# First attention of a two-layer kernel: VectorE's maxima over two banks at a time, a new order of the engines, and a re-ordered preparation

## Chip, core and metric

The kernel runs on one core of one Trainium2 chip. The metric is the device time of one execution in microseconds, the median of several runs. One further execution was recorded by the hardware profiler.

## What is computed

The reference is two transformer layers with cross-attention and feed-forward parts over x of 8 x 256 x 256 and a context of 8 x 1601 x 64. The change touches the first cross-attention alone:

```python
q_big  = rope(einsum('bshk,hkq->bshq', (x @ Wq.T).reshape(B, S, H, K), w_kc_q))   # H=16, K=128, q: 192
kv_r   = rope(kv_c)                                                               # 8 x 1601 x 64
q_r    = einsum('bshq,hqr->bhsr', q_big, W_qr)
k_r    = einsum('bld,hdr->bhlr', kv_r, W_kr)
scores = einsum('bhsr,bhlr->bhsl', q_r, k_r)
attn   = softmax(scores)
ctx_c  = einsum('bhsl,bld->bhsd', attn, kv_r)
out    = einsum('bhsd,hkd->bhsk', ctx_c, w_kc_kv) ... @ Wo.T
```

There are 8 batches x 16 heads = 128 heads, each with 256 query rows against 1601 keys. The kernel folds W_qr and W_kr into one matrix M per head, and w_kc_kv and Wo into one matrix per head (wvo).

## The kernel before

**Preparation** (`phase_prepare`). SP loads weights, x and the context. TensorE makes Wq x w_kc_q per head, transposes x, folds M and wvo. ScalarE copies results out of PSUM, takes the norms (lines 351 to 356) and splits weights into a high and a low float16 part. VectorE takes the largest absolute value of each batch of context (`top_of`, line 421), normalises x (lines 452 to 463), makes the low parts (`split_rest`, line 434) and applies the rotation to batches 5, 6 and 7 of the context (`turn_context`, lines 439 to 442); GpSimd rotates batches 0 to 4. VectorE's order at the end is: `split_rest` of 16 heads, the copy of the norms (line 482), `turn_context(5)`, the bounds and the scaling of M (line 494), the scale of the keys (lines 500 to 505), `turn_context(6)` and `(7)`. ScalarE takes the square root that normalises x after head 7 (line 356). SP stores M to DRAM in six pieces (lines 222 to 226), then wvo, 1 MB, to a DRAM scratch (line 231), and waits for that store (line 234) before the stage may end; all engines meet at the end of a stage.

**First attention** (`phase_attention0`). The order of every engine is written out by hand, in a loop over four heads, which is software-pipelined: while head n has its values summed, head n+1 has its scores made and head n+2 its maxima taken. Per head:

- TensorE, `maxima` (line 767): q (float16, 128 queries as weights) times all keys, in 4 chunks of 400 or 401 keys x 2 halves of the queries, 8 products, each into one of the two banks of `psM`, by turns. VectorE, `reduce_max` (line 1053), takes the maximum of each product: 8 reductions of 128x400. A product waits for the reduction two before it (`mx_done`), so one bank is filled while the other is read.
- VectorE, `join` (lines 1062 to 1070), joins the maxima into a column `mcol`; TensorE, `shift` (line 771), turns it by one 64-column transpose; ScalarE, `shift_copy` (line 935), puts it into rows of q2, so that the score products subtract it.
- TensorE, `scores` (line 783): 26 products of 256 columns in groups of 4, 4, 4 and 1 key tiles, into `psS[0]` and `psS[1]` by turns; the last group's tile has 65 keys, so its weights have 65 columns. ScalarE, `exp` (line 947), takes the exponential of a group. GpSimd (line 1152) makes the low part.
- TensorE, `values` (lines 801 and 804): 26 pairs of products of 129 and 65 columns, accumulated into `psV`; ScalarE copies it to `acc` (line 1002), SP stores it (line 684).
- Every two heads TensorE makes a new pair of queries: `q_first` (12 products, line 729), `q_second` (6), `q_lat` (float32, line 754), with the rotation by VectorE between them (lines 1012 to 1037), and the copies `q_high`, `q_other` (ScalarE, 923 and 930) and `q_low` (VectorE, 1044).

The transposed column and the joined maxima stand in the spare columns of `psM`'s second bank. Before the loop, the keys are transposed by TensorE (`turn_keys`, line 817) and copied by ScalarE (line 958), VectorE makes the values' low parts (`v_rest`, line 1076), and SP fills the buffers: `refill_maxima` is one DMA for each chunk (line 593). The rule that paces the maxima is this one:

```python
                if not (isinstance(n, int) and n == 0 and k < ST):
                    pe.wait_ge(mx_done, PASSES * n + k - 1)      # PASSES = 8, k = 0..7
```

## Time and profile before

| | us |
|---|---|
| three runs | 1766.52 to 1771.66, median 1769.66 |
| the profiled execution, its own time | 1781.06 |
| its span, first to last instruction | 1779.2 |
| first attention's loop, first to last copy of a head's result | 121.0 to 1193.3 |

| engine | busy us (share) |
|---|---|
| TensorE (PE) | 1653.8 (93%) |
| VectorE (DVE) | 1328.9 (75%) |
| ScalarE (ACT) | 1015.1 (57%) |
| GpSimd (POOL) | 925.9 (52%) |

PE is a matmul's record, PEld the load of its weights, SPq the SP engine's queue as it issues DMAs. A matmul's record runs from its start to the arrival of its last column, so records overlap: the pace of TensorE is read from start to start. A timeline row with "x6" merges six instructions, from the start of the first to the end of the last.

### The profile page before, as it was taken

The numbers are of one execution on the slowest core, as the hardware profiler recorded it, in microseconds if no ns is written. First come the engines' busy times: TensorE is split into PE (matmuls) and PEld (weight loads), VectorE is DVE, ScalarE is ACT, GpSimd is POOL, SyncE is SP. The second block draws the span as 40 slices with busy tenths as digits, with TensorE's granted clock in tenths as the row PEclk, the third lists the DMA queues.
The fourth block names the chain that finished last, engine by engine and source line by source line (L and its number), as shares of the span: only waits on it lengthen the run. The fifth ranks groups of instructions, "written<-read, shape, count | busy, mean of one in ns | idle before, by whom it ended". The sixth has DMA issues, their size and how long they took to land. (4 is left out here: it accounts for less than half of the span.)

```text
span 1779.2 us, 48732 instructions
## 1 busy us (share of the span) xinstructions
PE 1653.8 (93%) x16216; PEld 1326.5 (75%) x16216; DVE 1328.9 (75%) x2910; ACT 1015.1 (57%) x2028; POOL 925.9 (52%) x623
## 2 busy tenths in 40 slices
PE   5789999999999999999999999989777799987898
PEld 4568888888888888888888888868655455557776
DVE  5788888888888888888888888886564378874223
ACT  5676666666666666666666666652122266662111
POOL 5337777777777777777777777760002122111321
PEclk8699999999999999999999999999988899997999
DMA  9621121221221121121121142139300000004244
GB/s 261 232 80 51 58 85 50 58 81 50 61 77 53 57 83 52 58 83 52 55 83 53 52 128 79 56 98 315 92 11 23 21 13 12 12 7 172 93 140 146
DMA packets 150154, 144.14 MB, mean 81 GB/s; under 512 B 41306, under 2 KB 137224, under 8 KB 149600
## 3 DMA queue, kind: packets, MB, share of 16 engines
q1 hardware_dynamic: 148432, 139.56, 25.9%
q0 software_dynamic: 1536, 3.99, 0.6%
q8 instruction: 23, 0.38, 0.1%
q14 instruction: 19, 0.16, 0.0%
q10 hardware_dynamic: 144, 0.07, 0.0%
HBM read 91.61 MB, written 33.98 MB: 71 GB/s over the span
## 5 line engine op out<-in xcount | busy, mean ns | idle before, releaser
L1152 POOL TENSOR_TENSOR c_rest<-c_prob 128x1024 f16<-128x1024 f32 (+1 forms) x513 | 796.4, 1573 | 310.9 <-ACT c_prob L947 297.0
L947 ACT ACTIVATE c_prob<-c_psS,ln,c_exp_scale 128x1024 f32<-128x1024 f32 (+1 forms) x514 | 538.1, 1047 | 239.8 <-PE c_psS L783 234.7
L1053 DVE TENSOR_REDUCE c_mxp<-c_psM 128x1 f32<-128x400 f32 (+1 forms) x1040 | 589.4, 573 | 111.2 <-PE c_psM L767 97.0
L783 PE MATMUL c_psS<-c_q,c_kk 128*128 128x256 f16 (+1 forms) x3350 | 512.7, 273 | 0.2 <-issue 0.2
L801 PE MATMUL c_psV<-c_vb,c_prob 128*128 128x129 f16 (+1 forms) x3328 | 396.3, 222 | 0.0
L783 PEld LDWEIGHTS c_psS<-c_q,c_kk 128*128 128x128 f16 (+1 forms) x3350 | 321.9, 99 | 85.7 <-issue 0.4
L804 PE MATMUL c_psV<-c_vb,c_rest 128*128 128x65 f16 (+1 forms) x3328 | 374.1, 193 | 0.0
L767 PE MATMUL c_psM<-c_kkm,c_q 128*128 128x400 f16 (+1 forms) x1040 | 346.1, 333 | 4.8 <-DVE c_mxp L1053 3.0
L804 PEld LDWEIGHTS c_psV<-c_vb,c_rest 128*128 128x128 f16 (+1 forms) x3328 | 301.2, 99 | 22.1
L801 PEld LDWEIGHTS c_psV<-c_vb,c_prob 128*128 128x128 bf16 (+1 forms) x3328 | 305.2, 97 | 14.0
L729 PE MATMUL c_psQ<-c_xb,c_w2s 128*128 128x256 f16 x1188 | 164.1, 275 | 11.6 <-PEq L162 9.9
L1973 ACT ACTIVATE g_prob<-g_psS,g_bias 128x128 f32<-128x128 f32 (+1 forms) x264 | 107.0, 426 | 56.7 <-DVE g_bias L2014 56.7
L729 PEld LDWEIGHTS c_psQ<-c_xb,c_w2s 128*128 128x128 f16 x1188 | 102.9, 98 | 28.5 <-issue 12.7
L1835 POOL TENSOR_TENSOR g_km<-kT,g_hmask 128x1024 f32<-128x1024 f32 x18 | 34.0, 1912 | 157.8 <-PE g_psS L1874 120.1
L767 PEld LDWEIGHTS c_psM<-c_kkm,c_q 128*128 128x128 f16 x1040 | 101.7, 98 | 14.1 <-DVE c_mxp L1053 3.7
L754 PE MATMUL c_psQ<-c_roped,c_ms 128*128 128x256 f32 x396 | 101.5, 392 | 0.6 <-DVE c_roped L1037 0.6
L935 ACT ACTIVATE c_q<-c_psM 32x128 f16<-32x128 f16 x258 | 69.2, 268 | 48.9 <-PE c_psM L771 47.4
L2330 ACT ACTIVATE m_s<-m_psH 128x256 f32<-128x256 f32 (+1 forms) x48 | 18.4, 384 | 113.3 <-PE m_psH L2248 106.1
L923 ACT ACTIVATE c_q<-c_psQ 64x256 f16<-64x256 f32 x132 | 50.0, 379 | 49.9 <-PE c_psQ L754 48.3
L754 PEld LDWEIGHTS c_psQ<-c_roped,c_ms 128*128 128x128 f32 x396 | 70.0, 190 | 7.6 <-DVE c_roped L1037 0.8
L2366 DVE TENSOR_TENSOR m_g<-m_s,m_psH 128x256 f32<-128x256 f32 (+1 forms) x48 | 20.2, 420 | 72.8 <-ACT m_s L2330 68.0
L2014 DVE TENSOR_REDUCE g_bias<-g_psS 128x4 f32<-128x1024 f32 (+1 forms) x49 | 59.9, 1223 | 16.6 <-PE g_psS L1874 13.9
(298 smaller groups left out, 2153.6 us busy)
## 6 DMA issues: line engine op xcount, KB each, us to landing
c_w2s<-w_scr SPq DMA_DIRECT2D x66, 256.0 KB, 2.6
acc_scr<-c_acc SPq DMA_DIRECT2D x128, 129.0 KB, 2.2
c_ms<-m_scr SPq DMA_DIRECT2D x67, 192.0 KB, 2.3
c_w2s<-w_scr SPq DMA_DIRECT2D x66, 128.0 KB, 2.1
kv<-acc_scr SPq DMA_DIRECT2D x4, 2064.0 KB, 9.8
d_acc<-acc_scr SPq DMA_DIRECT2D x4, 2064.0 KB, 8.6
m_w<-in_L_ffn_W SPq DMA_DIRECT2D x16, 352.0 KB, 4.2
c_vb<-V SPq DMA_DIRECT2D x27, 129.0 KB, 2.0
```

Source lines behind the costliest of these rows:

```text
L729: mm = pe.matmul(out, weights[:, w, c], xb[:, x, c, :], start=(c == 0 and i == 0), stop=(c == DK - 1 and i == 2))
L754: mm = pe.matmul(psQ[:, S:2 * S], ms[:, e, :], roped[:, e, :], start=(e == 0), stop=(e == 2))
L767: pe.matmul(psM[:, st, 0:w], q1[slot][:, st * P:(st + 1) * P], kkm[:, c0:c0 + w], start=True, stop=True).then_inc(mx_full, 1)
L783: mm = pe.matmul(psS[g % 2][0:r, i * S:(i + 1) * S], src[:, (lo + i) * P:(lo + i) * P + r], mov[slot][:, :], start=(one == 0 and i % 2 == ...
L801: pe.matmul(psV[:, st * W:(st + 1) * W], high[0:r, c0:c0 + P], vb[0:r, i, :], start=(i == 0 and st == 0), stop=False, skip_group_check=True)
L804: mm = pe.matmul(psV[:, st * W + DC:(st + 1) * W], rest[g][0:r, c0:c0 + P], vb[0:r, i, DC:W], start=False, stop=(i == LT - 1), skip_group_ ...
L935: last = nc.scalar.activation(q2[slot][0:2 * SHIFT_ROWS, st * P:(st + 1) * P], shiftT[st * 2 * SHIFT_ROWS:(st + 1) * 2 * SHIFT_ROWS, :], A ...
L947: nc.scalar.activation(prob[g][0:r, 0:w], psS[g % 2][0:r, 0:w], ACT.Exp, bias=keep["ln1024"][0:r, :], scale=exp_scale[slot][0:r, :]).then_ ...
L1053: nc.vector.tensor_reduce(mxp[:, st, c:c + 1], psM[:, st, 0:CHUNKS[c][1]], AX.X, ALU.max).then_inc(mx_done, 1)
L1152: nc.gpsimd.tensor_tensor(rest[g][0:r, 0:w], prob[g][0:r, 0:w], high[0:r, 0:w], ALU.subtract).then_inc(rest_done, 1)
L1973: ins = nc.scalar.activation(prob[k % 2][:, i * w:(i + 1) * w], psS[k % 2][:, i * w:(i + 1) * w], ACT.Exp, bias=bias[k % 2][:, i:i + 1], a ...
L2014: nc.vector.tensor_reduce(bias[k % 2][:, 0:nh], psS[k % 2][:].rearrange("p (h k) -> p h k", h=nh), AX.X, ALU.max, negate=True).then_inc(bi ...
```

## The change

In the first attention a chunk of maxima is now two products, one into each bank of `psM`, and one reduction over both banks (4 for each head, of 128x2x400). A chunk's products wait for the reduction of the chunk before, so `psM` has no second buffer any more. The column and the joined maxima move to the second bank of `psS[1]`; `join` so waits for an exponential, and the first scores of a head wait for `shift_copy` themselves. The order of all engines in the loop is new. A refill of a chunk of keys is two DMAs of 64 partitions. In the preparation the wvo result stays in SBUF (no DRAM scratch), the square root follows head 3, `turn_context(5)` and the keys' scale come earlier, and the table load for the exponential moves to the end of the preparation.

```diff
@@ phase_prepare
-    wvo = sb("a_wvo", [P, H0 // 2, D])
+    wvo = keep["wvo_made"]
...
             sp.dma_start(keep["ms"][:], ...).then_inc(keep["in_m"], 16)
-            sp.wait_ge(vo_done, N_VO)
-            sp.dma_start(t["wvo_scr"], wvo[:]).then_inc(stored, 16)
...
-            sp.wait_ge(stored, 16 * 2)
+            sp.wait_ge(stored, 16)
...
-                if h == H0 // 2 - 1:
+                if h == 3:
                     act.wait_ge(var_ready, 1)
                     nc.scalar.activation(root[:], agg[:, :, 1], ACT.Sqrt, ...)
...
+            nc.scalar.activation(warm[:], eps[:], ACT.Exp)
...
             for h in range(H0):
                 split_rest(h)
+            turn_context(POOL_TURNS)
             n = D_NM
...
             dve.sem_inc(b2_ready, 1)
-            turn_context(POOL_TURNS)
+            dve.wait_ge(aall_ready, 1)
+            kscale = keep["kscale"]
+            link(nc.vector.tensor_reduce(ktop[:], aall[:], AX.X, ALU.max))
+            link(nc.vector.tensor_scalar(ktop[:], ktop[:], 1e-30, TURN_GROWTH / QK_TOP, ALU.add, ALU.mult))
+            link(nc.vector.reciprocal(kscale[:], ktop[:]))
+            link(nc.vector.tensor_copy(keep["k_unscale"][:], ktop[:]))
             dve.wait_ge(bound_ready, 1)
@@ phase_attention0
-    PASSES = 2 * len(CHUNKS)
+    PASSES = len(CHUNKS)
...
-    shiftT = psM[0:ST * 2 * SHIFT_ROWS, 1, SPARE:SPARE + P // 2].bitcast(F16)
-    mx = psM[:, 1, SPARE + P // 2:SPARE + P // 2 + ST]
+    shiftT = psS[1][0:ST * 2 * SHIFT_ROWS, 512:512 + P // 2].bitcast(F16)
+    mx = psS[1][:, 512 + P // 2:512 + P // 2 + ST]
...
-        queue.dma_start(kkm[:, c0:c0 + w], KK1[:, bass.ds(b * L + c0, w)]).then_inc(in_kkm[c], 16)
+        for half in range(2):
+            rows = slice(half * DC, (half + 1) * DC)
+            queue.dma_start(kkm[rows, c0:c0 + w], KK1[rows, bass.ds(b * L + c0, w)]).then_inc(in_kkm[c], 16)
...
-            def maxima(n, p, k, slot):
+            def maxima(n, p, c, slot):
...
-                    pe.wait_ge(mx_done, PASSES * n + k - 1)
+                    pe.wait_ge(mx_done, PASSES * n + c)
                 c0, w = CHUNKS[c]
-                pe.matmul(psM[:, st, 0:w], q1[slot][:, st * P:(st + 1) * P], kkm[:, c0:c0 + w], ...
+                for st in range(ST):
+                    mm = pe.matmul(psM[:, st, 0:w], q1[slot][:, st * P:(st + 1) * P], kkm[:, c0:c0 + w], ...)
+                mm.then_inc(mx_full, 1)
...
 def scores(n, g, slot, part=None):
+                    if g == 0:
+                        pe.wait_ge(shift_done, n + 1)
...
@@ TensorE's loop, the new order
+                    if u % 2 == 0:
+                        maxima(n + 1, p1, 3, s1)
+                        q_first(p, 0)
+                        scores(n, 2, u, (4, 8))
+                        values(n, 0, (0, 1))
+                        scores(n, 3, u)
+                        maxima(n + 2, p2, 0, s2)
+                        values(n, 0, (1, 2))
+                        values(n, 0, (2, 3), shift_of=n + 1)
+                        shift(n + 1)
+                        q_first(p, 1)
+                        values(n, 0, (3, 4))
+                        values(n, 1, (0, 1))
+                        maxima(n + 2, p2, 1, s2)
+                        values(n, 1, (1, 3))
+                        scores(n + 1, 0, s1)
+                        scores(n + 1, 1, s1, (0, 6))
+                        maxima(n + 2, p2, 2, s2)
+                        values(n, 1, (3, 4))
+                        scores(n + 1, 1, s1, (6, 8))
+                        values(n, 2, (0, 2))
+                        scores(n + 1, 2, s1)
+                        maxima(n + 2, p2, 3, s2)
+                        values(n, 2, (2, 4))
+                        values(n, 3)
+                    else:
+                        q_second(p)
+                        maxima(n + 2, p2, 0, s2)
+                        values(n, 0, (0, 2))
+                        scores(n, 3, u)
+                        values(n, 0, (2, 3), shift_of=n + 1)
+                        shift(n + 1)
+                        values(n, 0, (3, 4))
+                        values(n, 1, (0, 3))
+                        maxima(n + 2, p2, 1, s2)
+                        values(n, 1, (3, 4))
+                        scores(n + 1, 0, s1)
+                        values(n, 2, (0, 1))
+                        q_lat(p)
+                        maxima(n + 2, p2, 2, s2)
+                        scores(n + 1, 1, s1, (0, 2))
+                        values(n, 2, (1, 2))
+                        scores(n + 1, 1, s1, (2, 8))
...
+                        values(n, 3)
@@ ScalarE's loop
+                    exp(n, 2, u)
                     if u % 2 == 0:
-                        q_other((AHEAD // 2) * j + (u + 2) // 2, (u + 2) % AHEAD)
-                    exp(n, 2, u)
-                    shift_copy(n + 1, (u + 1) % AHEAD)
-                    exp(n, 3, u)
-                    exp(n + 1, 0, (u + 1) % AHEAD)
-                    if u % 2 == 1:
+                        shift_copy(n + 1, (u + 1) % AHEAD)
+                        exp(n, 3, u)
+                        exp(n + 1, 0, (u + 1) % AHEAD)
+                    else:
+                        exp(n, 3, u)
+                        shift_copy(n + 1, (u + 1) % AHEAD)
+                        exp(n + 1, 0, (u + 1) % AHEAD)
                         q_high((AHEAD // 2) * j + (AHEAD + u) // 2, u - 1)
...
+                    if u % 2 == 1:
+                        q_other((AHEAD // 2) * j + (AHEAD + u) // 2, u - 1)
@@ VectorE
-                nc.vector.tensor_reduce(mxp[:, st, c:c + 1], psM[:, st, 0:CHUNKS[c][1]], AX.X, ...
+                nc.vector.tensor_reduce(mxp[:, :, c], psM[:, :, 0:CHUNKS[c][1]], AX.X, ALU.max).then_inc(mx_done, 1)
...
+                    if u % 2 == 0:
+                        reduce_max(n + 1, 3)
                     join(n + 1)
+                    scale_of(n + 2, (u + 2) % AHEAD)
                     reduce_max(n + 2, 0)
...
@@ build
+        keep["wvo_made"] = sb(layer0, "wvo_made", [P, H0 // 2, D])
```

In the stage's start, the `v_rest(7)` of VectorE moves behind `join(0)`, the maxima of head 1 end with chunk 2, and `scores(0, 2)` stops after four products instead of six.

## Rows read from the trace of the kernel before

**Rows 1.** The page, part 1: busy time, share of the span, instructions.

```profile
PE 1653.8 (93%) x16216; PEld 1326.5 (75%) x16216; DVE 1328.9 (75%) x2910; ACT 1015.1 (57%) x2028; POOL 925.9 (52%) x623
```

**Rows 2.** Busy by stretch: us, PE, PEld, DVE, ACT, POOL, clock, DMA share, GB/s.

```profile
400.00:600.00 200.00, 200.00 (x2347) 168.25 (x2345) 172.52 (x404) 136.96 (x213) 147.28 (x96) 1.00 0.19 59
```

**Rows 3.** ScalarE's copy of a head's result: two of the timeline, then all.

```profile
129.75 0.38 ACT L1002 ACTIVATE c_acc<-c_psV 128x258 f32<-128x258 f32 x1
...
146.62 0.38 ACT L1002 ACTIVATE c_acc<-c_psV 128x258 f32<-128x258 f32 x1
...
L1002 ACT ACTIVATE c_acc<-c_psV x128: 375/377/379, 121.0 to 1193.3; 128x258 f32<-128x258 f32 x128
```

**Rows 4.** Groups by line, 600-1200 us: count | busy us, mean ns | idle.

```profile
L1053 DVE TENSOR_REDUCE c_mxp<-c_psM 128x1 f32<-128x400 f32 x422 | 238.6, 573 | 53.0 <-PE c_psM L767 46.2
...
L804 PE MATMUL c_psV<-c_vb,c_rest 128*128 128x65 f16 x1686 | 185.8, 193 | 0.0
...
L804 PEld LDWEIGHTS c_psV<-c_vb,c_rest 128*128 128x128 f16 x1686 | 152.3, 99 | 7.0
...
L783 PEld LDWEIGHTS c_psS<-c_q,c_kk 128*65 128x65 f16 x140 | 15.5, 112 | 0.8
```

**Rows 5.** The page, part 5: VectorE's reduction of 1024 columns, layer 1.

```profile
L2014 DVE TENSOR_REDUCE g_bias<-g_psS 128x4 f32<-128x1024 f32 (+1 forms) x49 | 59.9, 1223 | 16.6 <-PE g_psS L1874 13.9
```

**Rows 6.** Timeline of one head in the loop (start us, us, engine, line).

```profile
705.69 0.82 PE L729 MATMUL c_psQ<-c_xb,c_w2s 128*128 128x256 f16 x6
...
706.43 0.24 PE L771 MATMUL c_psM<-ident_sb,c_mcol 128*64 128x128 f16 x1
...
706.61 0.23 PE L801 MATMUL c_psV<-c_vb,c_prob 128*128 128x129 f16 x1
...
707.67 0.33 PE L767 MATMUL c_psM<-c_kkm,c_q 128*128 128x400 f16 x1
...
707.84 0.60 PE L783 MATMUL c_psS<-c_q,c_kk 128*128 128x256 f16 x4
708.04 2.96 DVE L1053 TENSOR_REDUCE c_mxp<-c_psM 128x1 f32<-128x400 f32 x5
```

**Rows 7.** Timeline of the stage's start, VectorE and TensorE.

```profile
98.34 1.05 DVE L1053 TENSOR_REDUCE c_mxp<-c_psM 128x1 f32<-128x400 f32 x2
...
98.96 0.34 PE L767 MATMUL c_psM<-c_kkm,c_q 128*128 128x400 f16 x1 [1.75 <-DVE c_mxp L1053]
```

**Rows 8.** Preparation, timeline: VectorE, ScalarE, SP queue; last, its wait.

```profile
19.06 1.17 DVE L455 BATCH_NORM_AGGREGATE a_agg<-a_stats 128x2 f32<-128x6 f32 x16
...
47.92 13.02 DVE L434 SCALAR_TENSOR_TENSOR a_wqk<-a_w,a_w_scale,a_wqk 128x384 f16<-128x384 f32 x24
63.57 0.17 DVE L482 COPY a_nsum<-a_psD 128x16 f32<-128x16 f32 x1 [2.63 <-PE a_psD L321]
...
68.47 2.29 DVE L494 TENSOR_TENSOR a_m<-a_m,a_m_scale 96x2048 f32<-96x2048 f32 x1
...
72.00 0.59 DVE L439 TENSOR_TENSOR a_rot<-kv,a_sink 128x416 f32<-128x416 f32 x1
...
77.43 1.03 DVE L442 TENSOR_TENSOR kv<-kv,a_rot 128x832 f32<-128x832 f32 x1
...
24.74 1.28 ACT L356 ACT_TABLE_LOAD   x1
...
81.87 3.65 ACT L951 ACTIVATE V<-kv,kscale 128x832 f16<-128x832 f32 x4 [9.02 <-PEq L162]
...
76.63 0.43 SPq L231 DMA_DIRECT2D wvo_scr<-a_wvo  x1
...
SPq L234 <- DMA wvo_scr<-a_wvo: 4.2, 1, 4.2
```

**Rows 9.** Timeline of the stage's start: the SP queue and TensorE.

```profile
87.87 2.49 SPq L593 DMA_DIRECT2D c_kkm<-KK  x4
...
94.70 1.47 PE L729 MATMUL c_psQ<-c_xb,c_w2s 128*128 128x256 f16 x12 [0.17 <-issue]
```

More of the change, by code:

```diff
@@ L723, in _, with q_rows @@
         def _(pe):
-            def q_rows(out, weights, maxima_of=None):
+            def q_rows(out, weights):
                 for c in range(DK):
                     for i, (w, x) in enumerate(((0, 0), (0, 1), (1, 0))):
-                        if maxima_of is not None and c == DK - 1 and i == 2:
-                            pe.wait_ge(mcol_done, 2 * maxima_of + 2)
                         mm = pe.matmul(out, weights[:, w, c], xb[:, x, c, :],
@@ L731, in q_rows, with q_first @@
                 return mm
-            def q_first(p, e, maxima_of=None):
+            def q_first(p, e):
                 if e == 0:
@@ L787, in scores, with values @@
                     mm.then_inc(s_full, 1)
-            def values(n, g, part=None):
+            def values(n, g, part=None, shift_of=None):
                 lo, hi = GROUPS[g]
@@ L795, in values @@
                     pe.wait_ge(rest_done, 4 * n + g + 1)
+                if shift_of is not None:
+                    pe.wait_ge(mcol_done, 2 * shift_of + 2)
                 high = prob[g][:].bitcast(BF16).rearrange("p (c t) -> p c t", t=2)[:, :, 1]
@@ L859, in _ @@
             turn_keys(15)
-            maxima(1, 0, 1, 1)
             pe.wait_ge(filled, 2)
@@ L866, in _ @@
             scores(0, 0, 0)
+            maxima(1, 0, 1, 1)
+            q_lat(1)
             maxima(1, 0, 2, 1)
-            maxima(1, 0, 3, 1)
-            q_lat(1)
-            maxima(1, 0, 4, 1)
             pe.wait_ge(k1_done, 16)
             scores(0, 1, 0)
-            maxima(1, 0, 5, 1)
-            maxima(1, 0, 6, 1)
-            maxima(1, 0, 7, 1)
-            scores(0, 2, 0, (0, 6))
+            scores(0, 2, 0, (0, 4))
             with pe.Fori(0, N // AHEAD) as j:
@@ L880, in _ @@
                     p = (AHEAD // 2) * j + (AHEAD + u) // 2
+                    p1 = (AHEAD // 2) * j + (u + 1) // 2
                     p2 = (AHEAD // 2) * j + (u + 2) // 2
                     s1, s2 = (u + 1) % AHEAD, (u + 2) % AHEAD
-                    scores(n, 2, u, (6, 8))
-                    scores(n, 3, u)
-                    values(n, 0, (0, 1))
                     if u % 2 == 0:
+                        maxima(n + 1, p1, 3, s1)
                         q_first(p, 0)
-                    maxima(n + 2, p2, 0, s2)
@@ L889, in _ @@
-                    values(n, 0, (1, 2))
-                    if u % 2 == 0:
-                        q_first(p, 1, maxima_of=n + 1)
-                    else:
-                        q_second(p, maxima_of=n + 1)
-                    shift(n + 1)
-                    values(n, 0, (2, 4))
-                    values(n, 1)
-                    maxima(n + 2, p2, 1, s2)
-                    scores(n + 1, 0, s1, (0, 4))
-                    maxima(n + 2, p2, 2, s2)
-                    scores(n + 1, 0, s1, (4, 8))
@@ L901, in _ @@
-                    maxima(n + 2, p2, 3, s2)
-                    scores(n + 1, 1, s1, (0, 2))
-                    values(n, 2, (0, 1))
-                    if u % 2 == 1:
-                        q_lat(p)
-                    maxima(n + 2, p2, 4, s2)
-                    scores(n + 1, 1, s1, (2, 6))
-                    maxima(n + 2, p2, 5, s2)
-                    scores(n + 1, 1, s1, (6, 8))
-                    values(n, 2, (1, 4))
-                    maxima(n + 2, p2, 6, s2)
-                    values(n, 3)
@@ L913, in _ @@
-                    scores(n + 1, 2, s1, (0, 6))
-                    maxima(n + 2, p2, 7, s2)
+                        scores(n, 2, u, (4, 8))
[7 more added lines that the diff above has]
+                        values(n, 0, (3, 4))
@@ L987, in _ @@
             exp(0, 1, 0)
+            q_other(1, 2)
             with act.Fori(0, N // AHEAD) as j:
@@ L1003, in _, with turn_first @@
                                          ACT.Copy).then_inc(pv_drained, 1)
+                    if u % 2 == 1:
+                        q_other((AHEAD // 2) * j + (AHEAD + u) // 2, u - 1)
         @block.vector
         def _(dve):
[L1007 to L1013 removed]
+            def turn_first(p, e):
+                if e == 1:
+                    dve.wait_ge(qA_full, p + 1)
+                    if not isinstance(p, int) or p > 0:
+                        dve.wait_ge(qk_full, p)
+                nc.vector.tensor_tensor(ropeB[:, 1 - e, :], psQ[:, e * S:(e + 1) * S],
+                                        tabB[:, e * S:(e + 1) * S], ALU.mult).then_inc(turnA, 1)
             def cos_first(p):
@@ L1061, in join @@
                 dve.wait_ge(mx_done, PASSES * (n + 1))
+                if not isinstance(n, int) or n > 0:
+                    dve.wait_ge(exp_done, 4 * n)
                 nc.vector.tensor_reduce(mx, mxp[:], AX.X, ALU.max).then_inc(mx_joined, 1)
@@ L1084, in _ @@
             dve.wait_ge(in_tab, 32)
-            turn_first(0)
+            turn_first(0, 1)
+            turn_first(0, 0)
             cos_first(0)
@@ L1112, in _ @@
             scale_of(1, 1)
+            v_rest(7)
             turn_second(1)
@@ L1115, in _ @@
             add_second(1)
-            for k in range(PASSES):
-                reduce_max(1, k)
+            reduce_max(1, 0)
+            reduce_max(1, 1)
+            reduce_max(1, 2)
             q_low(1, 2)
@@ L1130, in _ @@
                         cos_second(p)
-                    reduce_max(n + 2, 1)
-                    if u % 2 == 1:
                         add_second(p)
-                    for k in range(2, 6):
-                        reduce_max(n + 2, k)
+                        reduce_max(n + 2, 1)
+                        reduce_max(n + 2, 2)
+                        q_low(p, u - 1)
                     if u % 2 == 0:
-                        add_first(p)
-                    else:
-                        q_low(p, u - 1)
-                    reduce_max(n + 2, 6)
-                    scale_of(n + 2, (u + 2) % AHEAD)
-                    reduce_max(n + 2, 7)
+                        reduce_max(n + 2, 3)
         @block.gpsimd
```

101 lines of the change are left out of this document (38 added, 63 removed).

## The prediction

> **What bounds the kernel now.** I read the shares of the page first: TensorE is busy 93% of the span, VectorE 75% [rows 1]. Then the stretches: from 400 to 600 us TensorE is busy 200.00 of 200.00 us at a granted clock of 1.00, VectorE 172.52, ScalarE 136.96, GpSimd 147.28 [rows 2]. So in the first attention's loop VectorE, from which the change takes work, has slack, and TensorE has none. A busy TensorE may still wait inside its overlapping records, so I read the pace as well. Two heads take 146.62 - 129.75 = 16.87 us, and all 127 steps 1193.3 - 121.0 = 1072.3 us, that is 16.89 for two heads [rows 3]: hardly a refill of a batch costs anything. Against this stands what TensorE must stream. For one head: scores 26 x 256 columns, values 26 x (129 + 65), maxima 2 x 1601, queries 9 x 256 in float16 and, in float32, half of three products of 256, which pass four times (1536), the column 128: 18,870 columns, at 2.4 GHz 7.86 us, for two heads 15.73. The other 1.14 us are small: the 12 products of a key tile's values and their like follow at (707.67 - 706.61)/6 = 0.177 us for a tile's four products, where 2 x 194 columns are 0.162; and the 64-column transpose of the maxima costs 0.74 - 0.64 = 0.10 us before it and 0.18 - 0.05 = 0.13 behind it [rows 6]. The maxima's products already follow without a gap: 707.67, and the scores behind them at 707.84, 0.17 for 400 columns [rows 6]. No stall on VectorE is left to take away.
>
> **The maxima, VectorE.** Eight reductions of 573 ns [rows 4] become four over 802 elements. From 573 ns for 400 and 1223 ns for 1024 elements [rows 4, 5] one element costs 1.042 ns, so 802 take 0.99 us. For two heads 9.2 us become 7.9. On the critical path this is worth nothing: TensorE is the engine that never waits.
>
> **The maxima, TensorE.** The same eight products. What is new is the wait: both banks are filled, read, and only then filled again. How far apart must two chunks start? The second product starts 0.17 later and its record is 0.33 long [rows 6]: 0.50. VectorE starts 708.04 - 708.00 = 0.04 behind the end of a product [rows 6]; the reduction 0.99; TensorE starts 0.05 behind the end of one (the first of the two at 98.34 ends at 98.91, the product is at 98.96) [rows 7]. Sum 1.58 us. What the new order puts between chunks I add up from 0.109 us for a product of 256 columns ((0.60 - 0.27)/3), 0.177 for a tile of values, 0.65 for six query products and 0.34 for the chunk itself [rows 6]. In the even step: chunk 3 of the head before to chunk 0: 0.34 + 0.65 + 0.44 + 0.18 + 0.22 = 1.83; then 2.0, 2.2 and 1.9. In the odd step: 2.1, 2.9 and 2.3. The one tight place is from an even step's chunk 3 to the odd step's chunk 0: 0.34 + two tiles 0.35 + the last tile 0.18 + `q_second` 0.65 = 1.52, so TensorE waits 0.06 us. Everything behind it in its queue waits too, but only once in two heads: 64 x 0.06 = 3.8 us. The ends: nothing, if the reduction's end reaches TensorE earlier than its record says (two reductions end 1.05 after the first starts, not 1.15 [rows 7]), and 64 x 0.21 = 13.6 us, if the reduction over two banks costs 2 x 0.573 = 1.146. I take 3.8, since 128x1024 in one instruction is near and fits a line.
>
> **The other waits of the new order.** I walked each queue through two heads with these durations. `join` waits for the exponential of group 1, long done in both steps. Behind it on VectorE wait `scale_of` and the next reduction, whose slack is over 0.3 us. The wait for the column stands four value products ahead of the transpose, and `mcol` is there a tenth of a us earlier in the even step, more in the odd one. `shift_copy` is done half a us before the first scores, which now wait for it. `q_other`, behind the copy of the result, is done just before chunk 0 in the even step. GpSimd's order is unchanged and ahead. I cost all of these at nothing; their cover is between 0.1 and 0.5 us. If one goes, the next late thing is chunk 0, in every second head.
>
> **The 65-key tile.** Its two score products now stand behind short value products instead of behind products of 256 columns. Their loads of weights take 112 ns against 99 [rows 4]. Loads of 99 ns already hide behind products that follow 0.03 apart, so I take nothing; the bound from the rows is 128 heads x 0.014 = 1.8 us. The Trainium skill speaks against the change here (TensorE: Matmul & The Clock Gate, sections on LDWEIGHTS and on weight-path modes): the quick load needs 128 weight columns, any other takes columns / 1.2 GHz. By it 65 columns take 54 ns, about 27 more than a 65-column product hides, and the sum would be 3.5 us longer. The trace has the longer record, but no such load behind a short product.
>
> **The transpose.** It moves to another bank and other neighbours. Its gaps of 0.10 and 0.13 us stood there after products of 256 columns and before short ones [rows 6]; I leave them as they are: nothing. The bound below is that they go: 128 x 0.23 = 29 us.
>
> **The preparation.** The store of wvo is issued at 76.63, takes 0.43 to issue and 4.2 us of waiting: the stage ends at 81.26, and ScalarE starts the next at 81.87 [rows 8]. Without it the stage ends with VectorE, at 78.46: 2.8 us. Then VectorE itself gets shorter: `turn_context` takes (78.46 - 72.00)/2 = 3.23 us, and one of them moves into the 2.63 us in which VectorE waits between `split_rest`, which ends at 60.94, and 63.57 [rows 8]. New end: 64.17 + (78.46 - 63.57 - 3.23) = 75.8, that is 5.4 us before 81.26. The four scale operations that move with it fill the wait for ScalarE's root. SP is not later: from M's scaling (68.47 + 2.29 = 70.76) to 76.63 it needs 5.9 us [rows 8], and M is scaled some 2 us earlier, so it ends near 74.8. The root of x: its table load stands at 24.74, though the statistics are there at 20.23 [rows 8]. Up to 4.5 us could pass on; but ScalarE's norms, the loads of weights and VectorE's 13.02 us of `split_rest` follow, and I let 0.6 pass. The table load at the end is beside SP and VectorE. Preparation: -6.0 (from -2.8 to -9.9).
>
> **The stage's start and end.** Eight refills of 0.62 us in place of four stand in SP's queue before the next weights of the queries: 4 in 2.49 us now, so up to 2.5 us later, where `q_first` starts at 94.70 [rows 9]. Half of that is slack, and `v_rest(7)`, about 1 us, leaves VectorE's path before the column: together +0.3 (from -1.0 to +2.5). Two score products and two maxima less before the loop, which the last turn no longer does in surplus behind its last values: -0.6. At the seven changes of batch two more DMAs per chunk are asked for half a head or more before use: nothing. The wvo copy from SBUF is beside the loop: nothing.
>
> **Sum.** -6.0 + 0.3 - 0.6 + 3.8 = -2.5 us. The profiled execution took 1781.06 us with a span of 1779.2, so 1778.6 for one like it; against the median of 1769.66, 11.4 lower with the same program, 1767.2. What a measurement of this kernel can tell from no change is about 0.3%, 5.3 us.
>
> **The rivals.**
> (a) Faster. The wait of 0.06 us does not come up, and the early root passes up to 3 us more: -6.3 to -9.3, about 1762. For it: reductions pace faster than their records [rows 7]. Against: `split_rest` and the DMA of weights still stand behind the root. 0.28.
> (b) Much faster. The transpose's gaps are a hidden wait on the column, and with the wait four products ahead they go: -6.3 - 29, 1734, or part of it. Against: they are alike in both steps. 0.05.
> (c) Slower. Single buffering binds: between an even step's chunk 3 and the odd step's chunk 0, VectorE's reduction over two banks costs twice the old one, 1.146 us. Then 0.21 us are lost for two heads: -6.3 + 13.6 = +7.3, 1777. It decides from a stall of (5.3 + 6.3)/64 = 0.18 us, a reduction of 1.11 us, or one other hand-over 0.1 us longer. 0.15.
> (d) The freed VectorE time does nothing and the loop merely stands while the start gets shorter: the forecast. 0.52, between 1764.4 and 1775.
>
> The likeliest case is (d), 1767.2. The range reaches into (a) and (c) and leaves out (b) and the ends: 1760 to 1776.
>
> **What will show it.** Right: VectorE's reduction at 0.99 us x 516, its busy time some 80 us lower, TensorE's 16.8 to 16.95 us for two heads with one wait on `c_mxp` of 0.03 to 0.1 each second head; the first scores' stage starting near 76 instead of 81.9; no SP wait on wvo. Wrong: waits on the column or on the queries' copies in TensorE's list; a pace under 16.8, which would say that the gaps of the transpose were a wait; a next stage that starts at 78 or later.

## The result and the profile after

The changed kernel takes 1786.41 us, median of four runs (1784.18 to 1787.08). The kernel before, run beside it, takes 1769.3 (1766.52 to 1771.66). The ratio is 1.0089 with a 95% interval of 1.0077 to 1.0102: slower by 0.9%, about 16 us. The forecast was 1767.2, with 1776 as its upper end.

The page of the changed kernel, its busy time, and the copies of a head's result (shortest, median and longest in ns, then first and last start in us); they answer to [rows 1] and [rows 3]:

```profile
PE 1667.6 (93%) x16212; PEld 1334.0 (75%) x16212; DVE 1285.4 (72%) x2389; ACT 1003.7 (56%) x2030; POOL 928.3 (52%) x623
...
L1063 DVE TENSOR_REDUCE c_mxp<-c_psM 128x2 f32<-128x800 f32 (+1 forms) x519 | 514.9, 992 | 173.8 <-PE c_psM L763 170.1
...
L763 PEld LDWEIGHTS c_psM<-c_kkm,c_q 128*128 128x128 f16 x1038 | 81.1, 98 | 41.0 <-DVE c_mxp L1063 25.5
```

```profile
L1013 ACT ACTIVATE c_acc<-c_psV x128: 377/382/388, 115.3 to 1208.6; 128x258 f32<-128x258 f32 x128
```

VectorE is relieved, as intended. But the loop, from the first copy to the last, takes 1208.6 - 115.3 = 1093.3 us, where it took 1072.3 [rows 3]: 21.0 more, or 17.22 us for two heads in place of 16.89. It starts 5.7 us earlier (115.3 against 121.0). 21.0 - 5.7 = 15.3 us is nearly all of the difference of the medians. What lies behind the loop varies by some 14 us from one profiled execution to the next, though no kernel here changes what is computed there (585.9 us in that of before, 574.8 to 588.6 in the others). The loop repeats far better: 1072.1 to 1072.5 us in the three kernels that have the attention of before. So below I compare starts and loops, not spans.

The row of line 763 says where to look: TensorE's loads for the maxima stood idle 41.0 us, 25.5 of them for `c_mxp`, VectorE's maxima. The list of waits for 600 to 1100 us has the same (us, times, longest):

```profile
PEld c_psM L763 <- DVE c_mxp L1063: 10.1, 29, 0.4
```

29 waits in 500 us, or 29 times 17.22 us: one in two heads, 10.1/29 = 0.35 us each. That is how long the load of the weights waits; the product itself comes later by less, as the timeline shows. The timeline of an odd step shows it (TensorE's maxima in line 763, the two products of a chunk merged, `q_second` in line 727, VectorE's reductions in line 1063), with an untroubled chunk first:

```profile
697.63 0.50 PE L763 MATMUL c_psM<-c_kkm,c_q 128*128 128x400 f16 x2
...
698.16 0.99 DVE L1063 TENSOR_REDUCE c_mxp<-c_psM 128x2 f32<-128x800 f32 x1 [0.16 <-PE c_psM L763]
...
699.59 0.50 PE L763 MATMUL c_psM<-c_kkm,c_q 128*128 128x401 f16 x2
...
700.29 0.99 DVE L1063 TENSOR_REDUCE c_mxp<-c_psM 128x2 f32<-128x802 f32 x1 [0.54 <-PE c_psM L763]
...
700.45 0.82 PE L727 MATMUL c_psQ<-c_xb,c_w2s 128*128 128x256 f16 x6
...
701.34 0.51 PE L763 MATMUL c_psM<-c_kkm,c_q 128*128 128x400 f16 x2
```

`q_second`'s six products need 6 x 0.109 = 0.65 us, so chunk 0 could start at 701.10; it starts at 701.34, right behind the reduction's end at 701.28. **0.24 us are lost.** And the reduction itself is late: the products of an ordinary chunk end at 697.63 + 0.50 = 698.13 and VectorE starts at 698.16; those of chunk 3 end at 700.09 and VectorE starts at 700.29, 0.20 behind instead of 0.03.

In the even step chunk 3 has the same delay, and there the column is built from it:

```profile
691.51 0.51 PE L763 MATMUL c_psM<-c_kkm,c_q 128*128 128x401 f16 x2
...
693.82 0.19 PE L805 MATMUL c_psV<-c_vb,c_rest 128*128 128x65 f16 x1
693.94 0.23 PE L802 MATMUL c_psV<-c_vb,c_prob 128*128 128x129 f16 x1
694.01 0.19 PE L805 MATMUL c_psV<-c_vb,c_rest 128*128 128x65 f16 x1
...
694.09 0.19 PE L805 MATMUL c_psV<-c_vb,c_rest 128*128 128x65 f16 x1
694.22 0.24 PE L768 MATMUL c_psS<-ident_sb,c_mcol 128*64 128x128 f16 x1
694.39 0.83 PE L727 MATMUL c_psQ<-c_xb,c_w2s 128*128 128x256 f16 x6
```

```profile
692.23 0.99 DVE L1063 TENSOR_REDUCE c_mxp<-c_psM 128x2 f32<-128x802 f32 x1 [0.63 <-PE c_psM L763]
693.26 0.17 DVE L1073 TENSOR_REDUCE c_psS<-c_mxp 128x2 f32<-128x8 f32 x1
693.46 0.19 DVE L1078 TENSOR_SCALAR c_mcol<-c_psS 128x32 f16<-128x32 f32 x1
693.69 0.19 DVE L1081 SCALAR_TENSOR_TENSOR c_mcol<-c_psS,c_mcol 128x32 f16<-128x32 f32 x1
```

The products end at 692.02, the reduction starts 0.21 later, and the column is ready at 693.69 + 0.19 = 693.88. TensorE has reached the wait that stands four value products ahead of the transpose: line 805 starts at 693.82, the next product at 693.94 in place of 693.85, 0.09 us lost. The transpose (line 768) still has its own two gaps: 0.10 before it, (694.39 - 694.22) - 0.05 = 0.12 behind it.

The two stops are the whole loss: 63.5 x (0.24 + 0.09) = 21.0 us, what the loop is longer.

What differs for chunk 3 is in `reduce_max` and in what it becomes on VectorE:

```python
            def reduce_max(n, c):
                dve.wait_ge(mx_full, PASSES * n + c + 1)
                dve.wait_ge(in_kkm[(c + 1) % len(CHUNKS)], 32 * ((n + (c + 1) // len(CHUNKS)) // H0) + 32)
```

```
# VectorE's instructions as built, changed kernel, in the loop: chunk 2, then chunk 3
L1061 REGISTER_ALU
L1062 EVENT_SEMAPHORE                         [waits in_kkm3]
L1063 TENSOR_REDUCE c_mxp<-c_psM 128x2        [waits mx_full]
...
L1061 REGISTER_ALU
L1062 ISA (register operations)               [waits mx_full]
L1063 TENSOR_REDUCE c_mxp<-c_psM 128x2        [waits in_kkm0]
```

For chunks 0 to 2 the count of the keys' refill is 32 x (n // 16) + 32. Its wait is an instruction of its own, and it is over long before the products end (at 697.4, for the reduction at 698.16); the wait for the products stands on the reduction itself. For chunk 3 the count is 32 x ((n + 1) // 16) + 32. The instruction that works it out in registers carries the wait for the products, so it runs only when they are done, and the reduction stands behind it. The trace has it, on VectorE's own sequencer (DVEq), 128 times, once a head (shortest, median and longest in ns, then first and last start in us):

```profile
L1062 DVEq EVENT_SEMAPHORE  x391: 21/21/21, 88.0 to 1204.3; - x196
L1062 DVEq FUSED_REGOPS  x128: 112/115/122, 106.2 to 1199.7; - x128
```

In the odd step above it starts at 700.13, 0.04 us behind the end of the products at 700.09, takes 0.115 and ends before 700.25; the reduction starts at 700.29. So the 0.20 us are 0.04 to the register instruction, 0.115 for it and 0.045 from its end to the reduction.

### The profile page after: what moved, and what is told of

Read it like the earlier page. It is cut to its first block and busy times, and to the rows that moved or that the text cites. A ratio compares the mean times of both kernels' runs of the same rounds, so it can differ in the third digit from the quotient of the medians.

```text
span 1785.2 us, 47081 instructions
## 1 busy us (share of the span) xinstructions
PE 1667.6 (93%) x16212; PEld 1334.0 (75%) x16212; DVE 1285.4 (72%) x2389; ACT 1003.7 (56%) x2030; POOL 928.3 (52%) x623
## 5 line engine op out<-in xcount | busy, mean ns | idle before, releaser
L1063 DVE TENSOR_REDUCE c_mxp<-c_psM 128x2 f32<-128x800 f32 (+1 forms) x519 | 514.9, 992 | 173.8 <-PE c_psM L763 170.1
L782 PE MATMUL c_psS<-c_q,c_kk 128*128 128x256 f16 (+1 forms) x3348 | 481.2, 273 | 0.5 <-ACT c_q L944 0.5
L802 PE MATMUL c_psV<-c_vb,c_prob 128*128 128x129 f16 (+1 forms) x3328 | 434.6, 222 | 0.0
L805 PE MATMUL c_psV<-c_vb,c_rest 128*128 128x65 f16 (+1 forms) x3328 | 406.4, 193 | 0.0
L782 PEld LDWEIGHTS c_psS<-c_q,c_kk 128*128 128x128 f16 (+1 forms) x3348 | 289.6, 99 | 33.7 <-issue 0.7
L763 PE MATMUL c_psM<-c_kkm,c_q 128*128 128x400 f16 (+1 forms) x1038 | 261.8, 334 | 7.8 <-DVE c_mxp L1063 2.2
L763 PEld LDWEIGHTS c_psM<-c_kkm,c_q 128*128 128x128 f16 x1038 | 81.1, 98 | 41.0 <-DVE c_mxp L1063 25.5
L1013 ACT ACTIVATE c_acc<-c_psV 128x258 f32<-128x258 f32 x128 | 48.9, 382 | 62.6 <-PE c_psV L805 62.6
L944 ACT ACTIVATE c_q<-c_psS 32x128 f16<-32x128 f16 x258 | 67.9, 263 | 1.5
L1025 DVE TENSOR_TENSOR c_ropeB<-c_psQ,c_tabB 128x256 f32<-128x256 f32 x132 | 55.3, 420 | 17.0 <-PE c_psQ L727 17.0
```

Source lines behind the costliest of these rows:

```text
L763: mm = pe.matmul(psM[:, st, 0:w], q1[slot][:, st * P:(st + 1) * P], kkm[:, c0:c0 + w], start=True, stop=True)
L782: mm = pe.matmul(psS[g % 2][0:r, i * S:(i + 1) * S], src[:, (lo + i) * P:(lo + i) * P + r], mov[slot][:, :], start=(one == 0 and i % 2 == ...
L802: pe.matmul(psV[:, st * W:(st + 1) * W], high[0:r, c0:c0 + P], vb[0:r, i, :], start=(i == 0 and st == 0), stop=False, skip_group_check=True)
L805: mm = pe.matmul(psV[:, st * W + DC:(st + 1) * W], rest[g][0:r, c0:c0 + P], vb[0:r, i, DC:W], start=False, stop=(i == LT - 1), skip_group_ ...
L944: last = nc.scalar.activation(q2[slot][0:2 * SHIFT_ROWS, st * P:(st + 1) * P], shiftT[st * 2 * SHIFT_ROWS:(st + 1) * 2 * SHIFT_ROWS, :], A ...
L1063: nc.vector.tensor_reduce(mxp[:, :, c], psM[:, :, 0:CHUNKS[c][1]], AX.X, ALU.max).then_inc(mx_done, 1)
```

## The experiments

Theory: this arithmetic delays chunk 3's reduction by some 0.16 us, and the single buffer passes the delay on, to chunk 0 in the odd step and through the column in the even one. Rivals: the single buffer binds anyway; the new order costs TensorE time by its neighbours; the new preparation gives less than it seems. Each run's ratio is against the kernel before on the same chip. The loop is from the first to the last copy of a head's result; it holds 63.5 times two heads.

| kernel | ratio (95% interval) | loop, us | two heads, us |
|---|---|---|---|
| before | 1 | 1072.3 | 16.89 |
| changed | 1.0089 (1.0077 to 1.0102) | 1093.3 | 17.22 |
| e1_wait_order | 0.9998 (0.9988 to 1.0008) | 1075.6 | 16.94 |
| f1_late_before_chunk0 | 1.0047 (1.0024 to 1.0071) | 1086.8 | 17.11 |
| f2_late_before_column | 1.0033 (1.0019 to 1.0048) | 1081.3 | 17.03 |
| e7_half_reduction | 0.9935 (0.9916 to 0.9953) | 1070.2 | 16.85 |
| e4_chunk3_earlier | 0.9966 (0.995 to 0.9982) | 1070.3 | 16.86 |
| e2_preparation_alone | 0.9973 (0.996 to 0.9985) | 1072.5 | 16.89 |
| e8_wvo_kept_alone | 0.999 (0.9978 to 1.0001) | 1072.1 | 16.88 |
| e3_full_width_transpose | 0.9893 (0.9877 to 0.991) | 1053.1 | 16.58 |
| e6_wide_transpose_old_order | 0.9844 (0.9827 to 0.986) | 1052.9 | 16.58 |
| e5_wide_transpose_new_order | 0.9813 (0.9797 to 0.9829) | 1045.0 | 16.46 |

### The order of two waits

```diff
             def reduce_max(n, c):
-                dve.wait_ge(mx_full, PASSES * n + c + 1)
                 dve.wait_ge(in_kkm[(c + 1) % len(CHUNKS)], 32 * ((n + (c + 1) // len(CHUNKS)) // H0) + 32)
+                dve.wait_ge(mx_full, PASSES * n + c + 1)
```

> The changed kernel, with the two waits ahead of VectorE's reduction of a chunk in the other order: first the one on the refill of the keys (which is long satisfied), then the one on the products. Theory: in chunk 3 alone the refill's count has to be computed in registers between the wait on the products and the reduction, so that the reduction starts 0.20 us behind the products instead of 0.04. Then here it starts 0.04 behind them in chunk 3 too; TensorE's wait behind q_second falls from 0.24 to about 0.07 us, the wait for the column in the even step (0.09) goes, two heads take 16.95 instead of 17.22 us, and the time falls by some 17 us to about 1769. Rival: the hand-over of 0.20 belongs to chunk 3 itself (802 elements over two banks, what stands behind it): no change, 1786.

Measured: 1770.48 us. Its trace, TensorE and VectorE at the same place, and the list of waits of 600 to 1100 us:

```profile
690.82 0.50 PE L763 MATMUL c_psM<-c_kkm,c_q 128*128 128x401 f16 x2
...
692.41 0.51 PE L763 MATMUL c_psM<-c_kkm,c_q 128*128 128x400 f16 x2
```

```profile
691.36 0.99 DVE L1063 TENSOR_REDUCE c_mxp<-c_psM 128x2 f32<-128x802 f32 x1 [0.37 <-PE c_psM L763]
```

```profile
PEld c_psM L763 <- DVE c_mxp L1063: 5.6, 30, 0.2
```

The reduction now starts 691.36 - 691.32 = 0.04 behind the products, and chunk 0 starts 1.59 us after chunk 3 in place of 1.75. The order of two lines is worth 0.28 us for two heads, 17.7 us of the loop. The register instruction now runs at 689.5, before the products of chunk 3 are even started. The wait on the column is gone; what is left is chunk 0, 0.09 us late.

### Which of the two places costs what

The swap again, except in one reduction of chunk 3: in f1 the one that the odd step's chunk 0 waits for, in f2 the one that the column is joined from. There (`late=True`) the wait for the products stays first.

```diff
 # f1
                     if u % 2 == 0:
-                        reduce_max(n + 2, 3)
+                        reduce_max(n + 2, 3, late=True)
 # f2
                     if u % 2 == 0:
-                        reduce_max(n + 1, 3)
+                        reduce_max(n + 1, 3, late=True)
                     join(n + 1)
```

> The changed kernel with the two waits of the reduction swapped as in e1_wait_order, except in the one reduction of chunk 3 that the odd step's chunk 0 waits for (VectorE's last of the even step): there the wait for the products still comes first, so that VectorE computes the count of the other wait only after the products are done. Theory: this alone brings back the greater part: chunk 0 is late by 0.24 us in place of e1's 0.09, so two heads 16.94 + 0.15 = 17.09 us and the time 1770.5 + 10 = about 1780, with no wait on the column in the even step. Rival (the swap works in another way, by the other chunks or by the column alone): within 3 us of e1, about 1770.

> The mirror of f1_late_before_chunk0: only the reduction of chunk 3 that the column is joined from (VectorE's first of the even step) keeps the wait for the products first. Theory: TensorE then waits for the column ahead of the transpose in the even step (0.09 us in the changed kernel's trace) and chunk 0 of that step moves 0.16 later too, with little slack: 0.28 us (17.22 - 16.94) less f1's 0.15 is 0.13 at most, 0.09 at least, so two heads 17.03 to 17.07 and the time 1776 to 1779. The two additions of f1 and f2 over e1 should sum to the changed kernel's 16 us. Rival: chunk 0 alone is what matters, then within 2 us of e1.

Both ran on another chip, where the kernel before takes 1780.17; f1 took 1791.24 and f2 1786.76. Against e1's ratio they cost 0.49% (8.7 us) and 0.35% (6.2 us). The copies of a head's result and the waits of f1, then of f2:

```profile
L1013 ACT ACTIVATE c_acc<-c_psV x128: 375/382/388, 116.5 to 1203.3; 128x258 f32<-128x258 f32 x128
```

```profile
PEld c_psM L763 <- DVE c_mxp L1066: 10.5, 29, 0.4
```

```profile
L1013 ACT ACTIVATE c_acc<-c_psV x128: 375/382/388, 115.6 to 1196.9; 128x258 f32<-128x258 f32 x128
```

```profile
PEld c_psM L763 <- DVE c_mxp L1066: 5.4, 29, 0.2
```

Over e1 the loop is 11.2 us longer in f1 and 5.7 in f2, together 16.9 of the 17.7. The wait of some 0.35 us on `c_mxp` is back in f1 alone; f2's timeline has the stop four products ahead of the transpose instead, 0.08 us at 687.94. So two thirds go through chunk 0, one third through the column, at the lower end of what was expected of f2.

### Without the chain of the single buffer

```diff
-                nc.vector.tensor_reduce(mxp[:, :, c], psM[:, :, 0:CHUNKS[c][1]], AX.X, ALU.max).then_inc(mx_done, 1)
+                nc.vector.tensor_reduce(mxp[:, :, c], psM[:, :, 0:QL // 2], AX.X, ALU.max).then_inc(mx_done, 1)
```

This kernel takes the maxima of half the keys alone.

> The changed kernel, with its waits in their original order, but the reduction reads 200 columns of each bank in place of 400 or 401, so the maxima are those of half the keys alone. The reduction should take 0.57 us in place of 0.99. Theory (the loss is the chain of product, late start of the reduction, reduction, next product into the same two banks, 0.24 us in the odd step, and the column that comes from it 0.09 us late in the even step): both waits go, with 0.42 us to spare, two heads take 16.86 and the time is that of e4_chunk3_earlier, 1764 to 1767. Rival (the new order costs TensorE time by itself, through the neighbours of products or a transpose in another bank): two heads stay above 17.0 and the time above 1775, without a wait on the maxima.

Measured: 1762.84 us. A group of 600 to 1100 us:

```profile
L1063 DVE TENSOR_REDUCE c_mxp<-c_psM 128x2 f32<-128x400 f32 x237 | 136.3, 575 | 153.7 <-PE c_psM L763 152.8
```

The reduction takes 575 ns, no wait on it is left, and two heads take 16.85 us, with the late wait still in. So the chain of product, hand-over, reduction and next product holds all of the loss: 1093.3 - 1070.2 = 23.1 us. The rival that the order itself costs TensorE time falls; without its waits it is 0.03 us a pair faster than the old one (1070.2 us of loop against 1072.1 to 1072.5).

### Chunk 3 two products earlier

On top of e1, in the even step:

```diff
                         values(n, 2, (0, 2))
-                        scores(n + 1, 2, s1)
+                        scores(n + 1, 2, s1, (0, 6))
                         maxima(n + 2, p2, 3, s2)
+                        scores(n + 1, 2, s1, (6, 8))
                         values(n, 2, (2, 4))
```

> The first experiment, and in the even step chunk 3 of the maxima stands two score products (0.22 us) earlier. Theory: the 0.07 us that remain of TensorE's wait are the distance of the chunks alone, so they go, two heads take 16.87 to 16.90, and the time is 3 to 5 us below the first experiment, about 1765, 5 us below the kernel before. Rival: the chunk's own wait for VectorE's reduction of chunk 2 takes its place: no gain over the first experiment.

Measured: 1764.56 us, a loop of 1070.3, no wait of TensorE on the maxima. It removes the last 0.09 us, and the loop is as fast as with half the reduction. With the two edits the change gains what it could: 0.9966, and that is mostly the preparation.

### The preparation

e2: the attention of the kernel before, the preparation of the changed one. e8: of the preparation, only that wvo stays in SBUF.

> The kernel before with the changed preparation alone (wvo kept in SBUF, the root after head 3, turn_context(5) and the keys' scale earlier, the table load at the end); the first attention as before. Theory: the preparation is worth 5 to 6 us by itself, two heads stay at 16.87, the time is about 1763.5. Rival: the first copy of a result comes 5.6 us earlier in the changed kernel mostly through the new order of the stage's start: then less than 3 us here, 1767 or more.

> The kernel before, with one edit of the preparation: the wvo result stays in SBUF, so its store and the wait for it are gone; all else as before. Forecast on record for this part: the preparation's stage then ends with VectorE in place of the store, 2.8 us earlier, so 2 to 3 us off the time of the kernel before. Rival: nearly all of the 5 to 7 us that e2_preparation_alone gained comes from this store (then the same 5 us here), or none of it, because VectorE's end was the bound already (then within 1 us of the kernel before).

Measured: 1766.29 and 1769.95 us, in ratios a gain of 4.8 us (2.7 to 7.1) and of 1.8 (-0.2 to 3.9). The first instruction of ScalarE in the attention, 81.87 in the kernel before [rows 8], in e2 and in e8:

```profile
76.16 1.00 ACT L950 ACTIVATE V<-kv,kscale 128x832 f16<-128x832 f32 x1 [2.64 <-PEq L163]
```

```profile
79.30 3.64 ACT L949 ACTIVATE V<-kv,kscale 128x832 f16<-128x832 f32 x4 [4.95 <-PEq L162]
```

The whole re-ordering starts the stage 5.7 us earlier, the store alone 2.6. By time alone e8 can't be told from no change; by the trace it gives about half. The gain of e2 is just below the 5 to 6 us expected, which its interval includes. Its rival, that the changed kernel's early first copy comes from the new order of the stage's start, falls: with the old order there e2 has its first copy at 114.1, earlier still than the 115.3 of the changed kernel.

### The transpose's gaps

In the kernel before, the transpose widened from 64 to 128 columns (the added ones zero), its result on all partitions:

```diff
-    mcol = sb("c_mcol", [P, ST, 2 * SHIFT_ROWS], F16)
+    mcols = sb("c_mcol", [P, P], F16)
+    mcol = mcols[:, 0:ST * 2 * SHIFT_ROWS].rearrange("p (s r) -> p s r", s=ST)
...
-    shiftT = psM[0:ST * 2 * SHIFT_ROWS, 1, SPARE:SPARE + P // 2].bitcast(F16)
+    shiftT = psM[:, 1, SPARE:SPARE + P // 2].bitcast(F16)
...
-                pe.transpose(shiftT, mcol[:].rearrange("p s r -> p (s r)"), ident16[:]).then_inc(shift_full, 1)
+                pe.transpose(shiftT, mcols[:], ident16[:]).then_inc(shift_full, 1)
...
+            nc.vector.memset(mcols[:, ST * 2 * SHIFT_ROWS:P], 0.0).then_inc(zeroed, 1)
```

> The kernel before, with the column of maxima padded with zeros from 64 to 128 columns, so that its transpose has full-width weights and writes 128 partitions; the copies read the same rows. Theory: the gaps of 0.10 us before and 0.13 us behind the transpose come from its 64 columns, a narrower form than everything around it: they shrink to under 0.03 each, 128 x 0.2 = 26 us, time about 1743. Rival: the gaps belong to this transpose whatever its width (a wait on the column, the hand-over to a transpose): no change, 1769.

Measured: 1751.3 us, -1.1%, some 8 us above what was expected; a new stop, shown below with e6, takes about that back. The timeline of e3, TensorE around the transpose (line 772):

```profile
685.43 0.82 PE L730 MATMUL c_psQ<-c_xb,c_w2s 128*128 128x256 f16 x6
686.08 0.22 PE L772 MATMUL c_psM<-ident_sb,c_mcol 128*128 128x128 f16 x1
686.14 0.22 PE L802 MATMUL c_psV<-c_vb,c_prob 128*128 128x129 f16 x1
```

0.65 for six products, then 0.06 to the next: both gaps are gone, where they were 0.10 and 0.13 [rows 6]. They were neither a wait nor the transpose's work but its 64-column form among products of 128. Not every narrower form has them: the score products with weights of 65 columns stand among the same products without a gap (below, under the 65-key tile). The Trainium skill (TensorEngine Tiling (Array Packing), Key Properties) says that a change of the tiling mode drains TensorE. The gaps would fit that, 0.10 us before and 0.12 behind; but no run shows that a 64-column transpose changes the mode, only that the gaps go with its width.

Two more runs have the wider transpose: e5 on top of e4, e6 on top of e2.

> The kernel of e4_chunk3_earlier with the column's transpose 128 wide, as in e3_full_width_transpose. Theory (the 64-column form makes TensorE stop before and behind the transpose, 0.10 and 0.12 us for each head, and the new order has no other wait left): 16.86 - 2 x 0.22 = 16.42 us for two heads, 28 us less than e4's 1764.6, so about 1737. Rival (the values' low parts from GpSimd come too late once TensorE is faster, as the 0.14 us in front of one tile's products in e3 hints): the same wait stands behind this order's transpose, some 0.14 us a head or every second head are given back, 16.5 to 16.7, about 1745 to 1755, with a TensorE wait that ends by a GpSimd instruction.

> The kernel of e2_preparation_alone (the order of the kernel before, with the new preparation) and the transpose 128 wide. It tells whether the new order is worth anything once the transpose's gaps are gone. If the two gains simply add: 1766.3 - 20.2 = about 1746, with 16.56 us for two heads as in e3_full_width_transpose. If the new order of e5 is the better one, e5 is below this by (16.56 - 16.42) x 64 = 9 us; if it brings nothing, the two are within 2 us.

Measured: 1739.49 and 1744.88 us. In e5 no gap is left in either step; the transpose in its timeline (line 769):

```profile
691.86 0.19 PE L806 MATMUL c_psV<-c_vb,c_rest 128*128 128x65 f16 x1
691.89 0.22 PE L769 MATMUL c_psS<-ident_sb,c_mcol 128*128 128x128 f16 x1
691.94 0.22 PE L803 MATMUL c_psV<-c_vb,c_prob 128*128 128x129 f16 x1
```

16.46 us for two heads, near the 16.42 expected. Against e6, with the old order, the new one is worth 5.4 us of time and 7.9 us of loop, where 9 were expected. In the old order, e6, a new stop of 0.13 us stands in the odd step (TensorE, then GpSimd's low parts):

```profile
696.69 0.19 PE L804 MATMUL c_psV<-c_vb,c_rest 128*128 128x65 f16 x1
696.85 0.23 PE L801 MATMUL c_psV<-c_vb,c_prob 128*128 128x129 f16 x1
```

```profile
693.05 5.59 POOL L1152 TENSOR_TENSOR c_rest<-c_prob 128x1024 f16<-128x1024 f32 x3 [1.57 <-ACT c_prob L947]
```

GpSimd's second instruction of this stretch ends at about 693.05 + 2 x 5.59/3 = 696.78, and the values of its group start at 696.85 in place of 696.72. The same stop, 0.14 us, stands in e3. With the gaps gone the next late thing in the old order is GpSimd; in the new one it isn't. At 0.14 us for two heads this stop costs e3 some 9 us, about what its gain lacked. That the low parts are what TensorE waits for is read from these rows and wasn't tried by itself.

## Why the prediction was wrong

**What bounds the kernel** held: each stop of TensorE costs its length, and VectorE's freed time brings nothing.

**The maxima, VectorE** held: 992 ns against 0.99. Its busy time fell by 43.5 us, not some 80. By their records the reductions are shorter by about the amount forecast (128 x (8 x 0.573 - 4 x 0.992) = 79 us), but busy time counts an overlap of two records once, and before there was more of it: from 100 to 1150 us VectorE's groups add up to 943 us against 904.37 busy before, and to 862 against 843.89 after.

**The maxima, TensorE** is the step that failed, at the term "VectorE starts 708.04 - 708.00 = 0.04 behind the end of a product". It is right for chunks 0 to 2 (0.03 to 0.04) and was taken for chunk 3 too, where it is 0.20. So the stop is 0.24 us in place of 0.06. The rest of the step is right: with 0.04 the sum holds to 0.01 us (e1 has 1.59 us between the two chunks, forecast 1.58), and what TensorE has to do between them was forecast as 1.52 and is 701.10 - 699.59 = 1.51.

The row on which the term stood merges five reductions of chunks that aren't the last. Nor does it show a hand-over even for these, since VectorE was busy itself until 708.03; that 0.04 is right for chunks 0 to 2 is luck:

```profile
707.33 0.70 DVE L1017 TENSOR_TENSOR c_psQ<-c_psQ,c_tabA 128x512 f32<-128x512 f32 x1
```

The term for chunk 3 stood in the trace of before, a few rows further on. The product of its first half ends at 710.97 + 0.33 = 711.30, and VectorE starts at 711.52, 0.22 behind. The same register instruction is there, and the diff leaves the expression of the count, other than its factor, as it is:

```profile
710.97 0.33 PE L767 MATMUL c_psM<-c_kkm,c_q 128*128 128x401 f16 x1
...
711.52 0.57 DVE L1053 TENSOR_REDUCE c_mxp<-c_psM 128x1 f32<-128x401 f32 x1
```

```profile
L1051 DVEq FUSED_REGOPS  x160: 105/125/127, 114.9 to 1192.9; - x160
```

There it did no harm. In this step the next product of the maxima had the other buffer of `psM`; in the other step the register instruction runs at 703.3, while VectorE still works on `q_low` until 703.84.

**The other waits.** "I cost all of these at nothing" failed for the column. Its cover was put at a tenth of a us in the even step, and the same delay of 0.16 us used it up: 0.09 us stop. It was the same cause twice, and treating the places as independent hid that. f1 and f2 measure 11.2 and 5.7 us for the delay alone, where the sum had 3.8 for all; with it the two stops make 21.0.

**The 65-key tile** held. In the changed kernel its two products follow short value products: 702.04 in the odd step, 0.03 behind a product at 702.01 and 0.22 ahead of the next, which is two products' time:

```profile
702.01 0.19 PE L805 MATMUL c_psV<-c_vb,c_rest 128*128 128x65 f16 x1
702.04 0.39 PE L782 MATMUL c_psS<-c_q,c_kk 128*65 128x256 f16 x2
702.26 0.22 PE L802 MATMUL c_psV<-c_vb,c_prob 128*128 128x129 f16 x1
```

The longer load, 112 ns, costs nothing that can be seen. The rule of the Trainium skill (TensorE: Matmul & The Clock Gate, the sections on LDWEIGHTS and on weight-path modes) that would have made it 3.5 us is not borne out here.

**The transpose** held: its gaps are the same, 0.10 and 0.12, in another bank and with other neighbours. Rival (b), that they were a wait on the column, falls twice: they outlive the earlier wait, and they go with 128 columns. Most of the bound of 29 us was there to be had (e5 gains 0.40 us a pair over e4, 25 us of loop), by an edit that this change doesn't make.

**The preparation** held in its steps. VectorE's last instruction of the stage and ScalarE's first of the next:

```profile
74.83 1.02 DVE L442 TENSOR_TENSOR kv<-kv,a_rot 128x832 f32<-128x832 f32 x1
...
76.50 3.64 ACT L960 ACTIVATE V<-kv,kscale 128x832 f16<-128x832 f32 x4 [1.88 <-PEq L163]
```

VectorE ends at 75.85, forecast 75.8, and the stage starts 81.87 - 76.50 = 5.4 us earlier, forecast 5.4 and 0.6 for the root. From there to the first copy it was to take 0.3 us less (+0.3 - 0.6) and took 0.3 less, 38.8 in place of 39.1. Neither 0.6 nor 0.3 is shown by this: runs with the same preparation start the stage at 75.80 to 76.95, and runs with the same start of the stage take 38.0 to 40.2 us to the first copy.

**The rivals.** (c) came true: single buffering binds at the place it names, and by the way it gives as its third, "one other hand-over 0.1 us longer". The reduction at twice the old one, which it priced, did not happen. Its 13.6 us for 0.21 us of stop lacked the column and the 0.03 by which the stop is longer. At 0.15 its chance was small for what it hung on: a stop of 0.06 us is the difference of two sums of single rows, and one hand-over that is longer by 0.1 us counts 64 times. (a) needed that no stop comes up, which is e4: 1764.56, against its 1762. The forecast's range ended at 1776 by its trust in one hand-over, while the rival's own price reached 1777.

## What to carry to other kernels

When a change takes a double buffer away, the time from the last product over the reader's start and its end to the next product can become the critical path wherever the other work between two fills is about as short: there, read each hand-over for each iteration by itself, and read the reader's sequencer rows too, not only the engine's. Put the wait that comes last behind all others: what an engine has to compute for a wait's count should stand before the wait that holds it up. And a small gap that stands at the same place in every iteration on the bound engine can be the instruction's shape; widening it costs one run to try, and was worth more here (25 us) than the new order.

**The best version** is e5: the change, its two waits swapped, chunk 3 two products earlier, the transpose 128 columns wide: 1739.49 us, ratio 0.9813 (0.9797 to 0.9829), below both kernels.

## What the hardware showed beyond expectation

The count of chunk 3, with n + 1 divided by 16 in registers, costs VectorE's sequencer 112 to 122 ns in the changed kernel. Standing behind the wait for the products, it starts the reduction at 0.20 us behind them in place of 0.04; of the 0.16 us, 0.115 are the instruction and 0.045 the step from its end to the reduction. Ahead of that wait it costs nothing (e1). A transpose of 64 columns among products of 128 stops TensorE for 0.10 us before and 0.12 behind; with 128 columns it takes 0.05 to 0.06 us and stops nothing, and products with 65 columns of weights stop nothing either. What stays open: what in a 64-column transpose makes the gaps, and what the 0.03 us a pair are by which the new order, without its waits, is faster than the old.
